# Routed experts: dense sorted rows, weights as the stationary operand and copied by transfers, biases per partition

## The reference, cut to what matters

```
def experts(x):                      # x: layernormed; D = 256, F = 128, E = 16 routed, SH = 2 shared
    aff = sigmoid(x @ wa)            # [tokens, 16]
    topk_p, topk_i = top_k(aff, 2);  topk_p = topk_p / sum(topk_p)
    combine = sum(one_hot(topk_i) * topk_p[..., None], axis=2)
    y_e = (gelu(x @ g_e + gb_e) * (x @ w1_e + b1_e)) @ w2_e + b2_e        # of each expert e
    return x + sum of the shared y_e + sum over routed e of combine[e] * y_e
```

## Time and profile before

| | us |
|---|---|
| median of 3 runs (lowest, highest) | 1039.58 (1038.62, 1043.31) |
| span of the profiled execution | 1003.0 |
| PE busy | 931.1 |
| DVE busy | 706.4 |
| POOL busy | 653.7 |
| ACT busy | 577.5 |

### The profile page before, as it was taken

One profiled execution on the slowest core, in us unless ns is written; L12 is line 12 of the kernel. 1 busy time (PEld: TensorE's weight loads), 2 busy tenths in 40 slices (PEclk: granted clock), 3 DMA queues, 4 the chain that ended last, 5 costly groups with the idle time before them and its releaser, 6 DMA issues.

```text
span 1003.0 us, 22773 instructions
## 1 busy us (share of the span) xinstructions
PE 931.1 (93%) x9178; PEld 731.0 (73%) x9178; DVE 706.4 (70%) x1245; ACT 577.5 (58%) x909; POOL 653.7 (65%) x660
## 2 busy tenths in 40 slices
PE   8899999999999999999999998998888889999993
PEld 6678888888788888887887876666665457876661
DVE  4688888888897888888979665433667876465333
ACT  5898877787687777877866241221695454231221
POOL 4896779676876796778767646773266613306772
PEclk9999999999999999999999999999999898999997
DMA  3321121112111211121100932234122015142233
GB/s 120 122 76 66 53 75 54 55 63 74 43 64 54 74 54 54 64 74 43 34 23 14 289 118 79 85 81 152 52 53 64 22 33 164 48 125 79 87 84 126
DMA packets 62439, 77.59 MB, mean 77 GB/s; under 512 B 12504, under 2 KB 50488, under 8 KB 62330
## 3 DMA queue, kind: packets, MB, share of 16 engines
q1 hardware_dynamic: 54208, 61.69, 19.8%
q0 software_dynamic: 5952, 12.34, 4.6%
q10 hardware_dynamic: 2176, 2.10, 0.6%
HBM read 63.59 MB, written 12.51 MB: 76 GB/s over the span
## 4 chain that ended last, share of the span: by engine, by line
PE 62%; DVE 22%; ACT 7%; issue 4%; POOL 4%; DMA 1%; ACTq 0%; DVEq 0%; POOLq 0%
PE psum L785 22%; DVE arena L1896 7%; PE psum L1081 7%; PE psum L757 5%; PE psum L864 4%; PE psum L856 4%; PE psum L1100 4%; PE psum L909 3%; DVE arena L1933 3%; PE psum L1212 1%; PE psum L1078 1%; PE psum L1068 1%; PE psum L1017 1%; PE psum L1098 1%; DVE v L2299 1%
## 5 line engine op out<-in xcount | busy, mean ns | idle before, releaser
L785 PE MATMUL psum<-vT,split 128*128 128x512 f32 x1368 | 346.4, 402 | 7.6 <-DVE arena L1896 5.1
L1896 DVE SCALAR_TENSOR_TENSOR arena<-psum,arena 128x1023 f32<-128x1023 f32 (+2 forms) x208 | 265.6, 1277 | 76.3 <-ACT arena L1405 53.5
L785 PEld LDWEIGHTS psum<-vT,split 128*128 128x128 f32 x1368 | 248.4, 188 | 66.8 <-DVE arena L1896 7.3
L1405 ACT ACTIVATE arena<-psum,arena 128x512 f32<-128x512 f32 x160 | 109.1, 690 | 69.9 <-PE psum L785 69.0
L2451 POOL TENSOR_TENSOR split<-arena,split 128x256 fp32r<-128x256 f32 x114 | 83.6, 743 | 30.9 <-ACT split L1330 30.9
L1422 ACT ACTIVATE arena<-arena 128x1024 f32<-128x1024 f32 x80 | 84.4, 1058 | 32.6 <-POOL arena L2478 21.0
L2478 POOL TENSOR_TENSOR arena<-arena,v 128x1021 f32<-128x1021 f32 x32 | 76.4, 2389 | 40.3 <-DVE arena L1896 40.2
L757 PE MATMUL psum<-ident,arena 128*128 128x128 f32 x568 | 73.3, 274 | 9.2 <-POOL arena L2508 4.9
L2669 POOL DMA_INDIRECT bcast<-scratch_v,arena x62 | 60.7, 979 | 29.7 <-issue 11.9
L2676 POOL DMA_INDIRECT scratch_y<-bcast,arena x62 | 62.5, 1008 | 26.1 <-issue 16.1
L757 PEld LDWEIGHTS psum<-ident,arena 128*128 128x128 f32 x568 | 64.0, 141 | 21.2 <-POOL arena L2508 8.6
(11 more groups left out here) (275 smaller groups left out, 1816.5 us busy)
## 6 DMA issues: line engine op xcount, KB each, us to landing
bcast<-scratch_a SPq DMA_DIRECT2D x32, 512.0 KB, 3.7
arena<-in_w_a SPq DMA_DIRECT2D x16, 768.0 KB, 4.2
arena<-in_wout_a SPq DMA_DIRECT2D x8, 256.0 KB, 2.6
scratch_v<-v SPq DMA_DIRECT2D x8, 256.0 KB
arena<-scratch_y SPq DMA_DIRECT2D x8, 256.0 KB, 4.8
arena<-scratch_y ACTq DMA_DIRECT2D x8, 256.0 KB, 5.4
arena<-in_wg SPq DMA_DIRECT2D x4, 512.0 KB, 5.4
arena<-in_wu SPq DMA_DIRECT2D x4, 512.0 KB, 6.4
```

What stands on the lines that cost most here:

```text
L785: m = pe.matmul(bank, split[:, t % SPLITS, i, q, :], vT[:, j, q, half * BANK:(half + 1) * BANK], start=(n == 0), stop=(n == 3 * KD - 1))
L1405: act.activation(tile[:, hs], wide_of(t)[:, hs], ACT.Identity, scale=w[:, TAPS - 1:TAPS], bias=0.0).then_inc(sem["tap0"], 1)
L1896: dve.scalar_tensor_tensor(out=tile[:, s:T], in0=bank[:, 0:T - s], scalar=cw_a[:, j, i, TAPS - 1 - s:TAPS - s], in1=tile[:, s:T], op0=ALU. ...
```

## The change

What it does:

- The 2048 rows are gathered once each, in 16 gathers of 128, sorted and without padding, turned and laid side by side in SBUF (`hT_e`). A block is a stretch of 128 columns of this that begins at its expert's rows (`at_s`); a stretch may reach into the next expert's rows, whose results the next block overwrites.
- Up and down matmuls hold the weights as the stationary operand, 128 x 128, and move 128 columns of tokens. The result has the features on partitions, so biases are one value per partition: gelu's bias and the scalar of DVE's operation (`owned`, from two matmuls with the one-hot `whose`). The turn of the hidden tile and its copy go.
- The weights of a block are copied by a transfer of 384 KB inside SBUF into a ring of four slots (`ring_w`), on SP's queue (`copy_weights`). The source's address is dynamic.
- ACT writes a block's output to its place in `yT_e`, at a dynamic address. From block 15 on, PE turns finished pieces of 128 columns back (`turn_out`), DVE copies them (`rows_out`), and POOL scatters: 16 scatters.
- The down biases of all experts are added, weighted by the shares, to the shared experts' bank (`turn_shares`, `add_biases`), in float32; the shares are computed earlier. The filler matmuls before the lists go.
- In the first layer the preparation of the bf16 bias parts goes. The constants of the second layer (three copies of 256 KB, two of 1 MB) are issued between the ring's transfers of the first expert layer, after blocks 6, 8, 10, 13 and 18.

```diff
 # PE, for block j
-                    pe.matmul(up_bank, ones16[0:PARTS, :], bias_all[:, bass.ds(b, 2 * F)], start=True, stop=False, ...)
-                    for i in range(KD):
-                        m = pe.matmul(up_bank, hT_b[:, j % 2, i, :], arena[:, bass.ds(w + i * 2 * F, 2 * F)], ...)
+                    on.wait_ge(sem[f"ringw{j % RING}"], 16 * n_ringed(n, j))
+                    on.wait_ge(sem["blk_ht"], DENSE * n + min(j + 1, DENSE))
+                    if j >= 2:
+                        on.wait_ge(sem["blk_hid"], done + j - 1)
+                    for g in range(2):
+                        for i in range(KD):
+                            m = pe.matmul(bank[:, g * F:(g + 1) * F], slot_w[:, (2 * i + g) * F:(2 * i + g + 1) * F],
+                                          hT_e[:, i, bass.ds(at, P)], start=(i == 0), stop=(i == KD - 1), ...)
                     m.then_inc(sem["blk_up"], 1)
-                    pe.transpose(hid_bank, hid_b[:, j % 2, :], ident[:, :]).then_inc(sem["blk_v"], 1)
-                    pe.matmul(out_bank, ones16[0:PARTS, :], bias_all[:, bass.ds(b + 2 * F, D)], start=True, stop=False, ...)
-                    pe.matmul(out_bank, hidT_b[:, j % 2, :], arena[:, bass.ds(w + 2 * KD * F, D)], ...)
+                    on.wait_ge(sem["blk_hid"], done + j + 1)
+                    if j >= 1:
+                        on.wait_ge(sem["blk_y"], done + j)
+                    for dh in range(KD):
+                        at = 2 * KD * F + dh * P
+                        m = pe.matmul(out_bank[:, dh * P:(dh + 1) * P], slot_w[:, at:at + P], hid_b[:, j % 2, :], ...)
+                    m.then_inc(sem["blk_dn"], 1)
+                def turn_out(i):
+                    on.wait_ge(sem["blk_y"], BLOCKS * n + i + SETTLED + 1)
+                    on.wait_ge(sem["blk_r"], DENSE * n + i)
+                    for dh in range(KD):
+                        m = pe.transpose(row_bank[:, dh * P:(dh + 1) * P], yT_e[:, dh, i * P:(i + 1) * P], ident[:, :])
 # PE, the order
                 up(1)
+                turn_biases()
                 up(2)
                 down(0)
                 rank()
                 up(3)
                 down(1)
-                keep_busy(out_cols(6), BUSY_LIST)
+                turn_shares(0)
+                turn_shares(1)
+                add_biases(0)
                 members()
                 down(2)
                 down(3)
+                add_biases(1)
+                own_biases()
                 turn_in(0)
-                shared_bias()
                 turn_in(1)
                 for j in range(BLOCKS + 2):
...
-                    if 1 <= j <= BLOCKS:
-                        turn_hidden(j - 1)
-                    if j + 2 < BLOCKS:
-                        turn_in(j + 2)
-                    if j >= 2:
-                        block_down(j - 2, at.pop(j - 2))
+                    if j + 2 < DENSE:
+                        turn_in(j + 2)
+                    if j >= SETTLED + 2:
+                        turn_out(j - SETTLED - 2)
+                    if 1 <= j <= BLOCKS:
+                        block_down(j - 1)
 # SP
+            def copy_weights(n):
+                done = BLOCKS * n
+                on.wait_ge(sem["router"], n_router(n, "at_w"))
+                on.wait_ge(sem["wrt"], 16 * N_LOADS[n])
+                on.wait_ge(sem["proj"], n_proj(TILE_E[n] + 2 * SH - 1, 1))
+                for j in range(BLOCKS):
+                    if j % GROUPED == 0:
+                        ws = block_values(at_w, mybir.EngineType.SP, j, ...)
+                    if j >= RING:
+                        on.wait_ge(sem["blk_dn"], done + j - RING + 1)
+                    load(f"ringw{j % RING}", ring_w[:, j % RING, :], arena[:, bass.ds(ws[j % GROUPED], WORDS)])
+                    if n == 0 and j in CONSTANTS_AT:
+                        exponents_constants(CONSTANTS_AT.index(j))
 # ACT
-                    act.activation(gate_b[:, j % 2, :], up_bank[:, 0:F], ACT.Gelu).then_inc(sem["blk_gelu"], 1)
+                    act.activation(gate_b[:, j % 2, :], up_banks[j % 2][:, 0:F], ACT.Gelu,
+                                   bias=owned[:, 0, j:j + 1]).then_inc(sem["blk_gelu"], 1)
-                    act.copy(given[:, j % RING, :], out_bank).then_inc(sem["blk_y"], 1)
+                    act.copy(yT_e[:, :, bass.ds(at, P)], out_bank.rearrange("p (k t) -> p k t", k=KD)).then_inc(sem["blk_y"], 1)
 # DVE
-                    dve.tensor_tensor(hid_b[:, j % 2, :], up_bank[:, F:2 * F], gate_b[:, j % 2, :], ALU.mult)
+                    dve.scalar_tensor_tensor(out=hid_b[:, j % 2, :], in0=up_banks[j % 2][:, F:2 * F],
+                                             scalar=owned[:, 1, j:j + 1], in1=gate_b[:, j % 2, :], op0=ALU.add, op1=ALU.mult)
+                def rows_out(i):
+                    on.wait_ge(sem["blk_o"], DENSE * n + i + 1)
+                    if i >= RING:
+                        on.wait_ge(sem[f"sct{i % RING}"], 16 * n_given(n, i - RING, i % RING))
+                    dve.tensor_copy(given[:, i % RING, :], row_bank).then_inc(sem["blk_r"], 1)
 # POOL
-                for j in range(RING + 2):
-                    gather(j)
-                on.wait_ge(sem["router"], n_router(n, "result"))
-                for j in range(BLOCKS + 2):
-                    if j + RING + 2 < BLOCKS:
-                        gather(j + RING + 2)
-                    if j >= 2:
-                        scatter(j - 2)
+                for i in range(DENSE):
+                    gather(i)
+                on.wait_ge(sem["router"], n_router(n, "result"))
+                for i in range(DENSE):
+                    scatter(i)
```

More of the change, by code:

```diff
@@ L322 @@
 ROUTER = ["inc", "max1", "eq1", "key1", "km1", "one1", "aff2", "max2", "eq2", "key2", "km2", "one2", "mask"]
-ROUTER += ["up", "count", "by1", "by2", "by4", "ends", "starts", "place", "picked", "slot", "high", "base", "mark", "row", "hot0", "hot1"]
-ROUTER += ["second", "token", "nobody", "result", "before", "nth", "capped", "at_w", "at_b", "each", "sum", "share", "parts"]
+ROUTER += ["each", "sum", "share", "parts", "weighted", "weights", "members", "up", "count", "by1", "by2", "by4", "ends", "starts"]
+ROUTER += ["place", "picked", "slot", "high", "base", "mark", "row", "hot0", "hot1", "second", "token", "result"]
+ROUTER += ["before", "nth", "capped", "at_w", "whose", "spare", "skipped", "less", "from", "at_s"]
 FIELDS = ("dt", "t1", "hi", "cumlo", "tothi", "totlo", "t0", "t2", "t3", "lo", "cumhi", "wd", "dec")
@@ L452, in term_of @@
             return y2 if (j, i) == (0, LIGHT[1]) else term_a
[L455 to L461, removed]
+        STRETCH = DENSE * P + P
+        G_ = lay_out(w=EXPERTS * WORDS, hT=KD * STRETCH, rows=2 * F + D, gate_b=2 * F, wout=XT * D, yT=KD * STRETCH,
+                     hid_b=2 * F, mark=LISTS * DENSE // 2, aff=NC * E, key=NC * E, one=CHOICES * NC * E, mask=NC * E,
+                     S=NC * E, share_e=NC * EXPERTS, own=2 * LISTED, best=LISTS, km=NC, den=NC, share=LISTS, slot=LISTS,
+                     high=LISTS, base=LISTS, row=LISTS, nb=2 * (8 + E), pa=2 * (8 + E), pb=2 * (8 + E), st=E,
+                     spare=E, token=DENSE, result=DENSE, flag=DENSE)
+        assert EXPERTS * WORDS + KD * STRETCH + 2 * F + D + 2 * F == 18944
         w_e = G_["w"].rearrange("p (s n) -> p s n", s=EXPERTS)
@@ L2161, in shares @@
-                def shares():
-                    dve.reciprocal(G_["best"], G_["best"]).then_inc(sem["router"], 1)
-                    after("each")
-                    dve.tensor_tensor(G_["den"], best[:, 0], best[:, 1], ALU.add).then_inc(sem["router"], 1)
-                    after("sum")
-                    dve.reciprocal(G_["den"], G_["den"]).then_inc(sem["router"], 1)
-                    after("share")
-                    dve.tensor_tensor(share, best, G_["den"].unsqueeze(1).to_broadcast([P, CHOICES, NC]),
-                                      ALU.mult).then_inc(sem["router"], 1)
```

399 lines of the change are left out of this document (208 added, 191 removed).

## The result

The changed kernel takes 990.28 us (median of 4 runs, 988.01 to 994.44) against 1041.44 for the kernel before beside it (4 runs, 1038.62 to 1045.58): ratio 0.9539, interval 0.9503 to 0.9576.

What follows compares the result with a forecast made beforehand. PE was taken to set the pace of the expert loops. Stage changes of -11.3 and -14.6 us cut the span from 1003.0 to 977.1; keeping 36.6 above it gave 1013.7 us, range 1002 to 1036.

Steps and rivals of the forecast that it cites:

- the median of the three runs, 1039.58, lies 36.6 above the span, and I keep that: Whole kernel: 36.6 us between span and median time stay unchanged, added to the new span of 977.1.
- Gathers and scatters ... Worth 0 by itself: Expert loops: gathers and scatters fall from 31 to 16 each, worth 0, since PE waits for POOL only near the end.
- The round, 1.90: Expert loops: one block on PE falls from 2.44 to 1.90 us, giving -17.35 us a loop.
- lower end of 1.68: Expert loops: fastest round considered, 1.46 of matmul passes plus 0.22 of turns, without gaps.
- The ring, 3.4 us from slot to landing: Expert loops: a block's 384 KB weight copy takes 3.4 us including wait and gather, against 3.6 available.
- the prediction's own formula: Weights' ring: time between a slot's freeing and its use is two rounds less 0.2 us of matmul drain.
- the ring sets the round: Rival, expert loops: slot to landing takes 4.2 us, round 2.2, 18.6 us more, 1032; chance 20%.
- I am wrong if the round is above 2.1: Expert loops: the prediction's own failure sign, a round above 2.1 us, beside a time outside 1002 to 1036.
- Rival of half clock: Expert loops: waits for weights lower PE's clock in half the rounds, mean 2.75 us, 53 more, 1066; chance 12%.
- Constants, +3.3: First expert loop: second-layer constants on SP's queue, two 1 MB copies delaying weights by 1.65 us each; ends 0 and +8.
- Starts and ends: Around each expert loop: +2.0 us at the start (ends +1.0 and +4.0), +0.75 at the end (0 and +1.5).
- Weight loads: Rival, expert loops: loads before the 12 passes not hidden, round 2.74 us, 52 more, 1066; chance 3%; forecast took them as hidden.

Runs made afterwards that it cites:

- b_same: The kernel before, run again with no edit: 1036.29 us, ratio 0.9996; profiled execution 1038.05 us, span 1036.7.
- c_best_more_gathers: The changed kernel with five weight slots and constants after the first expert loop, plus 14 more gathers a stage of rows nobody reads: 1006.28 us.
- b_half_gathers: The kernel before with odd blocks taking the rows of the block before, so 16 gathers a layer instead of 31: 1004.59 us, ratio 0.9688.
- d_before_direct: The kernel before with odd blocks' rows loaded plainly on SP's queue, 128 neighbouring rows, instead of gathered by POOL: 1008.21 us, ratio 0.9727.

## Why the prediction was wrong

The forecast was 1013.7 us, faster, and the time is 990.3.

- **The step that failed: "the median of the three runs, 1039.58, lies 36.6 above the span, and I keep that".** It took for a fixed cost outside the span what was time inside the loops. Only 1.4 to 1.6 us lie outside a span (`b_same`: 1038.05 against 1036.7; the changed kernel: 991.27 against 989.7). The other 35 were inside the typical execution and missing from the profiled one: stops of the loops with half clock behind them (32.5 us in `b_same`). The change takes them away, since it gathers and scatters 16 times instead of 31. Half the gathers alone gave -32, and 14 more in the new kernel brought +34.
- **"Gathers and scatters ... Worth 0 by itself"** is the same error seen from the part. By the profiled execution it was right, POOL delays nothing there; in the typical one it was the largest gain of the change, and only the gap of 36.6 us between times and span pointed at it.
- **The round, 1.90.** PE's own is 1.56, below the lower end of 1.68: all the old gaps went, and four passes are 0.45 apart from the next group (633.97 to 634.42), 0.112 each and not 0.122. Without the ring 62 x 0.34 = 21 us would have come on top of the forecast.
- **The ring, 3.4 us from slot to landing.** Some transfers that PE waited for take that (issued at 617.11, used at 620.46), but others 4 to 6.5 us (issued at 626.22, used at 632.76), and there is no 0.2 us of slack against 1.56. By the prediction's own formula a mean round of 2.1 means 2 x 2.1 - 0.2 = 4.0 us from slot to use, an estimate. The mean round is 2.11 and 2.08: the rival "the ring sets the round" (2.2, given 20%) is what happened. The line "I am wrong if the round is above 2.1" is met in the first loop and nearly in the second. It cost about 26 us against no ring, and a fifth slot gets 15 back.
- **Rival of half clock.** It occurs behind some waits for the ring: PE was granted 0.50 for some 3 us behind the waits of 2.07 and 2.38 us (until 653.35 and 950.94), but not behind that of 2.04 (until 630.61). With the start of each loop this makes the mean clock 0.92 to 0.94, far from half of the rounds.
- **Constants, +3.3:** 2.9 in the traces of the first loop, 5.9 in the time; where the rest lies was not found.
- **Starts and ends:** +2.8 and +1.0 where +2.0 and +0.75 stood. Of the 5.8 between the loops (2.75 forecast) 1.7 lie between the last down matmul and the first use of the results, 1.5 ahead of the second loop; 2.6 arise between 767 and 865 in the second state-space layer, in lines that the diff does not touch: 2.9 us are gained there up to 811 and 5.5 lost behind it, and why was not found.
- **Weight loads:** hidden, as the earlier trace rows had it; 12 passes and two turns in 1.56 us leave no room for 12 x 0.192. By the ratio in the Trainium skill's "TensorE: Matmul & The Clock Gate", section "Back-to-back issue gap" (81 ns against 56), an estimate, the 12 passes alone would take 2.1 us. The trace does not agree: the whole round takes 1.56.

With the errors in the trace alone the time would have been missed the other way: span 989.7 instead of 977.1. Of these 12.6 us the two loops are 8.5 (the ring), the stretch between them 3.1, start and end 1.0. On the other side stand the 35 of the stops. So it is luck that the range was missed by 12 us and not by more: the two errors partly cancel. That the kernel gets faster was forecast for a reason that holds, the shorter loops, but most of the 51 us came from the part that the forecast put at 0.

**What stays open.** Why POOL's transfers hold up the engines behind PE was not seen. By the undisturbed length of the loops, 62 in 77.5 us (0.80 per us) and 46 in 57 do it, 47 in 77.5 (0.61) do not, and 32 in 57 hardly; a threshold was not sought, and gathers and scatters were not separated.

The traces suggest that runs of close transfers matter more than the mean rate. In `b_same` each of the eight runs of seven or eight indirect transfers less than 1.5 us apart ends in a wait of PE, of 0.7 us once and of 1 to 2 otherwise. In `c_best_more_gathers` most stops follow runs of five or six (the one shown above stands behind six, 650.42 to 656.90). In `b_half_gathers` and `d_before_direct` no run inside a loop is longer than three. But the first profiled execution of the kernel before has 48 in a row, 1.3 us apart, from 617 to 678, and no stop, and as many in its second loop. So a long run isn't enough, no experiment varied it alone, and why this execution was spared is not known.

## What to carry to other kernels

Before a profiled execution serves as the base, compare its span with the spread of the times: a gap that is not outside the span is in a stage, and a change may take it away. Here it was 35 us, more than the sum argued from the trace. And when a transfer is waited for in each round, give the ring one slot more than the mean latency asks: here one more slot of 384 KB gave 15 us.

## What the runs showed of the hardware

- POOL's indirect transfers, close together, made ACT, DVE and POOL start some 1 to 3 us late behind matmuls of PE ("remote"), whether or not anything needed their data. As many bytes by plain transfers cost 2.7 us instead of 34.
- Behind some idle times of 1.4 to 3.4 us PE was granted 0.50, for 3 us (`b_same`, from 956) to over 8 (from 997). Behind others it kept full clock (1.50 us until 944.14 in `b_same`, 2.04 until 630.61 in the changed kernel). The eight stops of `b_same` add up to 13 us and its loops are 32.5 longer, so a stop cost two to three times its length.
- A copy of 384 KB inside SBUF that PE waited for took 3.0 to 3.8 us from issue to use in the quickest cases of the changed kernel, up to 5.5 in its second loop, and up to 6.5 in the first, beside copies of constants.
